# Linear attention in a Perceiver block: query features as eight float32 tiles at once, unsplit queries, four feature banks, half of the attention moved among the key features

## The reference

```python
qkv = x @ w_qkv                                   # x: layer-normed, 512 tokens x 512
q, k, v = jnp.split(qkv, 3, axis=-1)              # each to 16 heads of 32
q_proj = _elu1(jnp.einsum('bhnd,hdf->bhnf', q, proj_matrix))   # _elu1(x) = x + 1 if x > 0 else exp(x)
k_proj = _elu1(jnp.einsum('bhnd,hdf->bhnf', k, proj_matrix))
kv = jnp.einsum('bhnf,bhnd->bhfd', k_proj, v)
attn = jnp.einsum('bhnf,bhfd->bhnd', q_proj, kv)
z = 1.0 / (jnp.einsum('bhnf,bhf->bhn', q_proj, k_proj.sum(axis=2)) + 1e-08)
out = (attn * z[..., None]) ... @ w_out + b_out
```

## Time and profile before

| | us |
|---|---|
| median of three runs | 700.75 |
| the profiled execution | 701.49 |
| span of the profiled execution | 699.7 |
| PE busy in the span | 660.3 (94%) |
| DVE busy | 318.4 (46%) |
| ACT busy | 251.1 (36%) |
| the list of the linear attention on PE, first projection of a query to last attention step | 317.2 to 377.6 |

### The profile page before, as it was taken

The page is one execution under the profiler, slowest core; times in us unless marked ns, Lnnn a source line. Parts: engine busy times, 40 slices in busy tenths (PEclk is TensorE's granted clock), DMA queues, the critical chain, the costliest instruction groups (busy, mean ns, idle before and its releaser), DMA issues.

```text
span 699.7 us, 10378 instructions
## 1 busy us (share of the span) xinstructions
PE 660.3 (94%) x4224; PEld 428.4 (61%) x4224; DVE 318.4 (46%) x646; ACT 251.1 (36%) x479; POOL 31.8 (5%) x33
## 2 busy tenths in 40 slices
PE   6989999999999999799998899989999999999967
PEld 5767778787777876578977485354544444444422
DVE  5964544536454354675877832423233231313301
ACT  4744545545354452455783213111220221121100
POOL 0300000000000000470000000000000000000000
PEclk9999999999999999899999969999999999999998
DMA  8111011010700000303076600889999999999931
GB/s 307 69 61 61 10 53 61 1 61 2 301 1 2 1 1 2 105 1 125 1 298 278 266 0 15 346 357 418 427 411 403 412 405 399 396 384 397 370 139 60
DMA packets 14347, 129.55 MB, mean 185 GB/s; under 512 B 2720, under 2 KB 2848, under 8 KB 6240
## 3 DMA queue, kind: packets, MB, share of 16 engines
q1 hardware_dynamic: 12848, 127.43, 46.2%
q10 hardware_dynamic: 1456, 1.49, 0.6%
HBM read 125.90 MB, written 1.05 MB: 181 GB/s over the span
## 4 chain that ended last, share of the span: by engine, by line
PE 82%; DVE 8%; ACT 4%; DMA 3%; SPq 2%; issue 1%; DVEq 0%; ACTq 0%
PE ps L1081 22%; PE ps L1348 15%; PE ps L1387 8%; PE ps L1358 6%; PE ps L1262 4%; PE ps L1151 4%; PE ps L1400 3%; PE ps L1226 3%; PE ps L1127 2%; PE ps L1162 2%; PE ps L1192 2%; PE ps L1299 2%; PE ps L1410 1%; PE ps L1311 1%; PE ps L1436 1%; DMA w_d<-in_wd 1%
## 5 line engine op out<-in xcount | busy, mean ns | idle before, releaser
L1387 PE MATMUL ps<-w_d,hid_T 128*64 128x512 f32 x256 | 58.2, 596 | 2.8 <-DMA w_d<-in_wd 1.5
L1348 PE MATMUL ps<-w_g,x_slot 128*64 128x512 f32 x256 | 58.1, 595 | 0.7 <-ACT x_slot L685 0.7
L1348 PE MATMUL ps<-w_u,x_slot 128*64 128x512 f32 x256 | 58.0, 595 | 0.0
L514 ACT ACTIVATE probs<-ps,neg_max 128x512 f32<-128x512 f32 x64 | 43.5, 687 | 39.1 <-DVE neg_max L795 39.1
L775 DVE COPY probs_T<-ps 128x512 f32<-128x512 f32 x32 | 22.1, 692 | 68.7 <-PE ps L1151 68.7
L651 ACT ACTIVATE hid<-ps 128x512 f32<-128x512 f32 x24 | 14.3, 598 | 108.7 <-PE ps L1348 79.8
L1081 PE MATMUL ps<-wv_hi,ctx_hi 128*128 128x512 f32 x128 | 51.7, 404 | 0.4 <-ACT v_s L495 0.4
L1081 PE MATMUL ps<-wv_lo,ctx_hi 128*128 128x512 f32 x128 | 50.0, 391 | 0.0
L1081 PE MATMUL ps<-wv_hi,ctx_lo 128*128 128x512 f32 x128 | 49.9, 390 | 0.0
L958 DVE TENSOR_TENSOR hid<-hid,ps 128x512 f32<-128x512 f32 x24 | 16.5, 687 | 69.6 <-PE ps L1348 39.6
L795 DVE TENSOR_REDUCE neg_max<-ps 128x1 f32<-128x512 f32 x64 | 39.8, 684 | 18.4 <-PE ps L1127 18.3
(11 more groups left out here) (218 smaller groups left out, 1218.0 us busy)
## 6 DMA issues: line engine op xcount, KB each, us to landing
w_u<-in_wu SPq DMA_DIRECT2D x16, 2048.0 KB, 16.7
w_d<-in_wd SPq DMA_DIRECT2D x16, 2048.0 KB, 12.8
w_g<-in_wg SPq DMA_DIRECT2D x16, 2048.0 KB, 13.2
ctx_raw<-in_ctx SPq DMA_DIRECT2D x7, 1024.0 KB, 4.7
w_qkv<-in_wqkv SPq DMA_DIRECT2D x1, 3072.0 KB, 15.3
ws_g<-in_wsg SPq DMA_DIRECT2D x1, 2048.0 KB, 7.7
ws_u<-in_wsu SPq DMA_DIRECT2D x1, 2048.0 KB, 8.0
ws_d<-in_wsd SPq DMA_DIRECT2D x1, 2048.0 KB, 21.3
```

Source lines behind the costliest of these rows:

```text
L514: act.activation(probs[:, p, :], bank(SCORE[p]), ACT.Exp, bias=neg_max[:, p:p + 1], scale=1.0, accum_out=row_sum[:, p:p + 1]).then_inc(exp ...
L1348: ins = pe.matmul(ps[64 * fh:64 * (fh + 1), dst, :], x_slot[:, e, dt, :], weights[e % 2][:, dt, BANK * fh:BANK * (fh + 1)], start=(dt == 0 ...
L1387: ins = pe.matmul(ps[64 * fh:64 * (fh + 1), 6 + n % 2, :], hid_T[:, n % 2, j, 64 * fh:64 * (fh + 1)], w_d[e % 2][:, KT * fh + j, :], start ...
```

## The change

Five things change at once.

1. The queries are no longer split. ACT copies the projection once, 128x512, to `q_l`; DVE has no part in it.
2. A step `("q", i, 0)` computes the four units of query tile i together, as eight float32 products of 32 rows by 64 columns of weights (line 1307 of the kernel after), into four banks; the steps with r from 1 to 3 do nothing on PE. The weights are a second copy of the projection matrix, `proj_rows`, brought by four more transfers. The group waits until all four banks are free.
3. The feature units use a table of banks: u % 3 for the first eight, then four banks (2, 0, 1, 7) in turn.
4. ACT computes the relu of every second unit throughout (16 units; before it was 24), DVE does the other 16 itself. ACT's exponential of unit u waits for DVE's unit u - 3.
5. LIN_ORDER is a new list. Key tiles 0 and 1 come first, without kv steps among them; then query tile 0, four kv steps, query tile 1, four kv steps; then key tiles 2 and 3 with an attention step of the first eight heads after each two units; then query tile 2, four kv steps, query tile 3, four kv steps, and the other four attention steps. The attention steps use banks 5 and 6, but for two of the last four (3 and 4).

A head's block in `v_bd` and `kv` is 44 wide instead of 48. The lines of SP and its wait for all 16 kv steps are unchanged.

```diff
-KVW = 48
+KVW = 44
...
-        LIN_ORDER = [("p", 8, 0), ("k", 0, 0), ("k", 0, 1), ("p", 9, 0), ("k", 0, 2), ("k", 0, 3), ("p", 10, 0), ("p", 11, 0)]
-        for ahead, behind in ((("k", 1), ("kv", 0)), (("k", 2), ("kv", 1)), (("k", 3), ("kv", 2)),
-                              (("q", 0), ("kv", 3))):
...
+        LIN_ORDER = [("p", 8, 0)] + four("k", 0) + [("p", 9, 0)] + four("k", 1) + [("p", 10, 0), ("p", 11, 0)]
+        LIN_ORDER += four("q", 0) + four("kv", 0) + four("q", 1) + four("kv", 1)
+        for t in range(NT):
+            LIN_ORDER += four("k", 2 + t // 2)[2 * (t % 2):2 * (t % 2) + 2] + [("att", 0, t)]
+        LIN_ORDER += four("q", 2) + four("kv", 2) + four("q", 3) + four("kv", 3) + four("att", 1)
+        UNIT = {step: u for u, step in enumerate(step for step in LIN_ORDER if step[0] in "kq")}
+        FEAT_BANK = [u % 3 if u < 8 else (2, 0, 1, 7)[u % 4] for u in range(len(UNIT))]
...
+        def att_first(a):
+
+            return 3 if a in (5, 7) else 5
+
         def act_relus(u):
-
-            return u % 2 == 0 or u >= NT * KT
...
+            return u % 2 == 0
...
+            for j in range(HPT):
+                src = proj_d[j % 2].rearrange("d (i u) f -> d i u f", u=2)
+                sp.dma_start(proj_rows[HD * j:HD * (j + 1)], src[:, :, j // 2, :]).then_inc(proj_rows_in, 16)
...
+                    if u >= 3:
+                        act.wait_ge(feat_done, u - 2)
+                    act.activation(exps[:, u % 3, :], bank(FEAT_BANK[u]), ACT.Exp).then_inc(fexp_done, 1)
...
-                    heads_high(i, ql_halves, i - 8)
+                    act.wait_ge(qkv_ps, i + 1)
+                    act.copy(q_l[:, i - 8, :], bank(qkv_bank(i))).then_inc(qkv_act, 1)
...
-                        dve.wait_ge(kv_ps, NT * (i - 1))
+                        dve.wait_ge(kv_ps, NT * (i - 2) + r + 1)
...
-                elif kind == "p":
-                    heads_low(i, ql_halves, i - 8)
...
+                elif kind == "q":
+                    if r == 0:
+                        qkv_out(8 + i)
+                        if i == 0:
+                            pe.wait_ge(proj_rows_in, 16 * HPT)
+                        for j in range(HPT):
+                            feature_bank_free(u + j)
+                        for j in range(HPT):
+                            dims = slice(HD * j, HD * (j + 1))
+                            for side in range(2):
+                                feats = slice(64 * side, 64 * (side + 1))
+                                ins = pe.matmul(ps[feats, FEAT_BANK[u + j], :], proj_rows[dims, i, feats],
+                                                q_l[dims, i, :], start=True, stop=True)
+                            ins.then_inc(feat_ps, 1)
+                    u += 1
...
                     for done in kv_done:
-                        pe.wait_ge(done, NT * KT // 2)
-                    pe.wait_ge(feat_done, 16 + 8 * (i + 1))
-                    if a >= 2:
-                        pe.wait_ge(att_done, a - 1)
+                        pe.wait_ge(done, NT * (i + 1))
+                    pe.wait_ge(feat_done, UNIT["q", 2 * i + 1, HPT - 1] + 1)
+                    before = max((c for c in range(a) if att_first(c) == att_first(a)), default=None)
+                    if before is None:
+                        qkv_out(10)
+                    else:
+                        pe.wait_ge(att_done, before + 1)
```

More of the change, by code:

```diff
@@ L114, in perceiver_block @@
         v_bd = sb(linear, "v_bd", [P, NT, H, 2, KVW])
-        rows = ExitStack()
-        att = sb(rows, "att", [P, NT, D])
-        att_T = sb(rows, "att_T", [P, KT, TOK])
-        rows.close()
-        ql_halves = sb(linear, "ql_halves", [P, KT, 2, TOK], F32R)
+        proj_rows = sb(linear, "proj_rows", [P, KT, FEAT])
+        first = ExitStack()
+        q_l = sb(first, "q_l", [P, KT, TOK])
+        xn_lo = sb(first, "xn_lo", [P, KT, TOK], F32R)
+        first.close()
+        att_T = sb(linear, "att_T", [P, KT, TOK])
+        att = sb(linear, "att", [P, NT, D])
         bout_rows = sb(linear, "bout_rows", [P, D])
@@ L289, in perceiver_block, with four, unit_of_bank_before @@
         ATT_BANK = (0, 1, 2, 7)
[L294 to L308 removed]
+        def four(kind, i):
+            return [(kind, i, r) for r in range(NT)]
+        LIN_ORDER = [("p", 8, 0)] + four("k", 0) + [("p", 9, 0)] + four("k", 1) + [("p", 10, 0), ("p", 11, 0)]
[5 more added lines that the diff above has]
+        FEAT_BANK = [u % 3 if u < 8 else (2, 0, 1, 7)[u % 4] for u in range(len(UNIT))]
+        def unit_of_bank_before(u):
+            return max((v for v in range(u) if FEAT_BANK[v] == FEAT_BANK[u]), default=None)
+        def att_first(a):
+            return 3 if a in (5, 7) else 5
+        def act_relus(u):
+            return u % 2 == 0
+        QKV_BY = [("dve",)] * 4 + [("act", "dve")] * 4 + [("act",)] * 4
         SHARED = [("s", i) for i in range(NF)]
@@ L600, in _ @@
                     act.wait_ge(feat_ps, u + 1)
-                    act.activation(exps[:, u % 3, :], bank(u % 3), ACT.Exp).then_inc(fexp_done, 1)
+                    if u >= 3:
+                        act.wait_ge(feat_done, u - 2)
+                    act.activation(exps[:, u % 3, :], bank(FEAT_BANK[u]), ACT.Exp).then_inc(fexp_done, 1)
                     if act_relus(u):
-                        act.activation(relus[:, u % 3, :], bank(u % 3), ACT.Relu).then_inc(frelu_done, 1)
+                        act.activation(relus[:, u % 3, :], bank(FEAT_BANK[u]), ACT.Relu).then_inc(frelu_done, 1)
                     u += 1
@@ L1266, in _, with feature_bank_free @@
                 qkv_project(n)
+            def feature_bank_free(u):
+                before = unit_of_bank_before(u)
+                if before is None:
+                    qkv_out(11 if FEAT_BANK[u] == 7 else 4 + FEAT_BANK[u])
+                else:
+                    pe.wait_ge(feat_done, before + 1)
             u = w = a = 0
@@ L1287, in _ @@
                         for part in range(2):
-                            ins = pe.matmul(bank(u % 3), proj_parts[part][:, 2 * i + r // 2, r % 2, :],
-                                            ql_halves[:, i, r // 2, :], start=(part == 0), stop=(part == 1))
+                            ins = pe.matmul(ps[:, FEAT_BANK[u], 2 * FEAT * pr:2 * FEAT * (pr + 1)],
+                                            kl_halves[:, i, pr, P * r:P * (r + 1)],
+                                            proj_parts[part][:, 2 * i + pr].rearrange("p h f -> p (h f)"),
+                                            start=(part == 0), stop=(part == 1))
```

40 lines of the change are left out of this document (11 added, 29 removed).

## The result

| | before | after |
|---|---|---|
| median, us | 700.45 (4 runs, 699.08 to 702.2) | 726.48 (4 runs, 725.55 to 727.39) |
| span of the profiled execution | 699.7 | 725.6 |
| mean granted TensorE clock | 0.976 | 0.953 |
| busy PE / DVE / ACT | 660.3 / 318.4 / 251.1 | 675.3 / 314.5 / 244.6 |

The account below looks back on a forecast made before the run. PE was taken to set the time up to the last kv step. The fourth addition 18.7 us later, plus 0.9, gave 19.6 us: 720.3 against the median of 700.75; own range 717 to 723.5, wider range 710 to 729.

Parts of the forecast that it names:

- The method, laying the list out by the rows' durations: Stage's new list priced from traced durations and waits: three stretches sum to 61.4 us, last kv step at about 378.9.
- the four query stretches: Each query tile with its four kv steps: 4.3 us of work, 2.5 of PE waits, 6.75 in all; four make 27.0.
- the term of 9.4: End of the stage: 390.2 instead of 380.85, 9.4 us later, although PE has less to do.
- The group of eight: Query features as eight 32-row products: 1.04 us to the next product, saving PE 3.9 us over four groups.
- Rival D: Query groups: the eight products do not overlap, 7 us a group against 1.04, 735 us in all; chance 0.02.
- The load of `ws_d`: Behind the stage: released by the last kv step, lands 22.6 us later at 401.5; ACT waits 11.3 us.
- Rival A: Behind the stage: the list waits as laid out but the loads are not late, only 9.4 us remain, 710.2; chance 0.08.
- C: Stage: PE stays the bound, never stopped by a copy, so not slower, 701.9 us; chance 0.04.
- the clock inside the stage: PE's granted clock in the stage: assumed to stay at 1.00, as in the window with 23.39 of 27.09 us busy.
- rival B: PE's clock falls inside the stage: 727 us, or 736 with key units and attention also at half clock; chance 0.13.
- The sum of the fourth addition: DVE's fourth addition behind the stage: could start at 414.4 against 395.71 before, 18.7 us later.
- The 0.9 for the last w_out product at 1.2 GHz: Behind the stage: PE's last-tile product takes 7.2 us instead of 3.6; two thirds of 1.3 counted, bounds 0 and 1.3.

Follow-up runs that it names:

- e1: The changed kernel with products that nobody reads filling the places where PE waits; 720.83 us, ratio 1.0291.
- e2: The changed kernel with the `ws_d` load issued second of the four instead of fourth; 721.94 us, ratio 1.030.
- e3: The changed kernel with both edits, PE's gaps filled with unused products and `ws_d` issued second; 710.92 us, ratio 1.014.
- e5: The changed kernel's new forms (groups of eight, unsplit query, four feature banks) with the old list of the kernel before; 714.65 us, ratio 1.0184.
- e7: The changed kernel with an alternating list that fits the new forms, ACT taking two relus of three, `ws_d` loaded second; 703.14 us, ratio 1.0036.
- e8: e7 with banks 3 and 4 given to the first and third of the last four attention steps; 696.25 us, ratio 0.9922.
- e11: The kernel before with five unused products where PE waits for the last normalised tile, behind the stage; 696.89 us, ratio 0.9952.

## Why the prediction was right, and where it was short

- The method, laying the list out by the rows' durations: right. The waits before query tile 0 were 2.44, 1.03 and 0.77 for 2.3, 1.1 and 0.9; the attention steps 3.64 apart for 3.65; before the third and fourth kv step 1.58 and 0.55 for 1.6 and 0.9. Counted from the start of the stage it was 2.0 us short: with the clock held (e1) the last kv step came after 63.7 us, and 61.7 were forecast (its three stretches, 61.4, give 378.6; the prediction wrote 378.9). The whole 2.0 lies in the four query stretches, which took 7.2 to 7.3 us each in e1 for 6.75 (and 7.3 in e2 without filling, 335.53 to 342.86): the third kv step starts 4.65 us behind the group (337.15 to 341.80) and not 4.3. So the term of 9.4 was 11.4 where ACT could begin its split (75.0 us from the start of the stage in e1 and e3, 63.6 in the kernel before), and 10.2 in the time of e3.
- The group of eight: 1.05 us for 1.04. Rival D, that the eight don't overlap, is out. Every wait inside the query stretches was ended by ACT or DVE. The Trainium skill, "TensorEngine Tiling (Array Packing)", section PSUM Bottleneck, says that tiling makes PE's part quicker and not the emptying of the banks; the trace agrees.
- The load of `ws_d`: the mechanism right, its landing 23.4 us behind the last kv step for 22.6, and by e1 against e3 it costs 9.9 us of its own. Rival A, loads not late, is out, and so is C: PE was busy for 58.6 of 70.2 us up to the last kv step, not bound.
- The step that failed is the clock inside the stage, taken as 1.00. It was 0.83 up to the last kv step, which ended at 385.9: 8.6 us later than 378.9 less the 1.6 of the earlier start, 6.5 of them the clock (70.2 against the 63.7 of e1) and 2.0 the query stretches. The measured 726.48 lies outside the forecast's own range (717 to 723.5); only the wider range, which keeps the lower half of rival B, holds it. Rival B named just this and priced it from 727; I gave it 0.13, on the ground that 23.39 busy of 27.09 us had gone at 1.00. That was the wrong row to lean on: a mean over 27 us says nothing of its longest gap, and the new stretches had PE busy for 1.32 of 3 us. With the earlier trace rows (0.47 busy of 3 us, then 0.53) in hand, B deserved far more than 0.13.
- What the clock cost up to the last kv step arrived in full, through the load. What it cost behind it did not: the last four attention steps took 13.11 us instead of 7.42 (e1), but ACT's wait for the load hid that and shrank from the 11.3 laid out to 6.1. The sum of the fourth addition: 414.4 laid out, +7.0 for the last kv step, +0.8 for the landing, -0.1 for a first addition 2.46 instead of 2.56 behind ACT's split, -0.2 for tiles 3.38 instead of 3.45 apart, is 421.9, as measured.
- The 0.9 for the last w_out product at 1.2 GHz: measured 0, and not the 1.3 either that the prediction weighed beside it. The product took 3.60 us, as in the earlier trace rows: the stage ended so late that PE still had three tiles of w_out to do from 403.40 on, and was idle for only 1.36 us afterwards. In e1 it ran dry, as laid out:

```profile
408.63 1.12 PE L1366 MATMUL ps<-ident,xn_moe 128*128 128x128 f32 x4 [7.49 <-DVE xn_moe L733]
409.54 5.75 PE L1231 MATMUL ps<-w_out,att_T 128*128 128x512 f32 x8
```

The product then took 5.75 us, and still the fourth addition came 3.52 us behind the third instead of 3.38: even there the term is 0.1.

## What to carry to other kernels

When a change takes work off the engine that is always busy, ask first which other engine empties its banks, and behind how many items the emptying stands; a group that needs four banks at once turns their spread into one long gap. A gap of PE costs itself and can cost the clock of what follows: here a gap that shrank by 1.3 us was worth 6.9, while the attention steps with a gap of 0.7 us before each kept the upper level. And a load released by a step moves with the step: when the list is reordered, look at who waits for its last transfer.

## What the runs showed of the hardware

- The granted clock fell to its lower level (1.2 GHz) inside a stage in which PE was busy for 83% of the time (58.58 of 70.23 us). In the stretches before or around the falls it had been busy for 1.32 of 3 us (changed kernel), 2.21 of 7 (e5) and 4.64 of 7 with a gap of 2.49 (e7). It did not fall in e8 with 5.99 of 7 and a gap of 1.21, nor inside the stage in e1 and e3, with unused products in the gaps.
- It also fell with PE busy for 4.00 of 4 us, behind 48 products of 32 columns in a row (e11).
- Where it falls varies between executions: with the same instructions of PE up to there, 337:358 went at 0.67 in the changed kernel and at 0.92 in e2. e2's four runs spread over 9.5 us, while kernels with filled gaps spread over 2.4 (e1, e3).
- Eight products of 32 rows and 64 columns take 1.05 us to the next full-width product even where neighbours in the list use the same 32 rows, which the earlier trace rows left open, and 1.94 at the lower level (345.36 to 347.30), both in the changed kernel.
- The last of four 2 MB loads, issued within 1.9 us, landed 23.4 us behind the last kv step, and the same load issued second 12.4 us behind its issue (e2).
